# Gate weights split in their natural layout and turned by 48 DMA transposes instead of by TensorE

## The reference

```python
x = x + xattn(layernorm(x), ctx, Wq, Wkv)            # 128 context rows for each batch, one head of width 512
x = x + ffn(layernorm(x), w_gate, w_up, w_down)

def ffn(x, w_gate, w_up, w_down):                    # the inner width is 1536
    x = act_qdq(x)                                   # scale = max|x| / 32767 over the WHOLE tensor, round, clip
    up = act_qdq(x @ lpbq_dequant(w_up).T)
    gate = act_qdq(x @ lpbq_dequant(w_gate).T)       # weights: blocks of 32, 15 levels, dequantised
    sig = fixed_qdq_u16(sigmoid(gate))
    gate = act_qdq(gate * sig)
    o = act_qdq(gate * up)
    return o @ lpbq_dequant(w_down).T
```

## Time and profile before

| | us |
|---|---|
| three runs | 890.88, 889.6, 889.14 (median 889.6) |
| the profiled execution | 889.12 |
| its span | 887.3 |
| PE busy | 858.3 (97% of the span) |
| DVE, ACT, POOL busy | 689.5, 585.5, 195.4 |
| L1043, the gate matmuls, on the chain of waits | 130.05 to 316.69 |

### The profile page before, as it was taken

How to read it: one execution, slowest core, us unless ns; L and a number is a source line. 1 busy time by engine, 2 the same in 40 slices (tenths; PEclk the granted TensorE clock), 3 DMA queues, 4 the chain that set the end, 5 groups by cost and what they waited for, 6 DMA issues and landing times.

```text
span 887.3 us, 11953 instructions
## 1 busy us (share of the span) xinstructions
PE 858.3 (97%) x4108; PEld 424.5 (48%) x4108; DVE 689.5 (78%) x965; ACT 585.5 (66%) x712; POOL 195.4 (22%) x170
## 2 busy tenths in 40 slices
PE   7999969999999999999999999999899989999998
PEld 5877544444444444444444444444444434444443
DVE  4879885566647459689998987584999997999892
ACT  2468776785655366599999987752889965455430
POOL 0099948399300295000000000000000000000000
PEclk9999989999999999999999999999999999999999
DMA  9822228766989549999779964997998887989872
GB/s 348 339 84 109 107 83 288 232 169 188 304 252 313 196 156 238 270 379 371 261 258 341 334 236 161 357 378 262 323 406 271 277 319 273 374 299 401 316 294 96
DMA packets 118402, 236.56 MB, mean 267 GB/s; under 512 B 47952, under 2 KB 57168, under 8 KB 116304
## 3 DMA queue, kind: packets, MB, share of 16 engines
q1 hardware_dynamic: 117200, 231.77, 74.0%
q10 hardware_dynamic: 1152, 4.19, 1.2%
HBM read 130.55 MB, written 95.42 MB: 255 GB/s over the span
## 4 chain that ended last, share of the span: by engine, by line
PE 71%; DVE 9%; POOL 8%; issue 6%; DMA 3%; SPq 1%; ACT 1%; DVEq 0%; ACTq 0%; POOLq 0%
PE ps L1106 28%; PE ps L1043 21%; PE ps L1159 13%; PE ps L1059 4%; PE ps L1186 4%; DVE big L1960 3%; DVE big L1953 3%; POOL big L875 2%; DMA big<-in_L_ffn_w_gate_dram 2%; POOL big L832 1%; POOL big L826 1%; PE ps L1176 1%; POOL small L872 1%; DMA big<-up_park 1%; POOL big L830 1%
## 5 line engine op out<-in xcount | busy, mean ns | idle before, releaser
L1106 PE MATMUL ps<-big 128*128 (+1 forms) x1152 | 248.8, 379 | 0.0
L1204 ACT ACTIVATE big<-ps 128x1024 f32<-128x1024 f32 (+2 forms) x154 | 126.4, 830 | 147.7 <-PE ps L1043 62.5
L1043 PE MATMUL ps<-big 128*128 (+1 forms) x864 | 186.6, 379 | 0.7 <-DVE big L1736 0.7
L1106 PEld LDWEIGHTS ps<-big 128*128 128x128 f16 x1152 | 112.7, 98 | 135.9
L1043 PEld LDWEIGHTS ps<-big 128*128 128x128 f16 x864 | 84.4, 98 | 102.7 <-issue 0.9
L1159 PE MATMUL ps<-big 128*128 128x512 f16 x576 | 125.1, 379 | 3.2 <-DVE big L1981 3.2
L817 POOL PARTITION_ALL_REDUCE small<-small x8 | 2.9, 368 | 451.6 <-DVE small L1922 170.1
L1781 DVE TENSOR_REDUCE small<-big 128x1 f32<-128x1024 f32 x36 | 43.8, 1218 | 71.0 <-ACT big L1204 71.0
L1159 PEld LDWEIGHTS ps<-big 128*128 128x128 f16 x576 | 56.2, 98 | 71.6 <-issue 2.9
L1140 PE MATMUL ps<-big 128*128 128x512 f16 x384 | 84.2, 379 | 4.3 <-ACT big L1489 4.3
L1874 DVE TENSOR_REDUCE small<-big 128x1 f32<-128x1024 f32 x48 | 58.2, 1215 | 13.7 <-ACT big L1204 13.6
(11 more groups left out here) (118 smaller groups left out, 1222.3 us busy)
## 6 DMA issues: line engine op xcount, KB each, us to landing
big<-up_park SPq DMA_DIRECT2D x90, 512.0 KB, 6.7
big<-gate_park SPq DMA_DIRECT2D x48, 512.0 KB, 6.3
up_park<-big SPq DMA_DIRECT2D x48, 512.0 KB, 4.1
gate_park<-big SPq DMA_DIRECT2D x36, 512.0 KB, 2.7
sign_park<-big SPq DMA_DIRECT2D x36, 256.0 KB, 2.7
big<-in_x_dram SPq DMA_DIRECT2D x8, 1024.0 KB, 18.5
x_park<-big SPq DMA_DIRECT2D x8, 1024.0 KB, 3.9
product_park<-big SPq DMA_DIRECT2D x16, 512.0 KB, 3.5
```

The source lines that it names most:

```text
L1043: mm = nc.tensor.matmul(unit_banks(n)[:, j], WG[:, x, a, k % 2, o:o + P], XT[:, g, b, k], start=(k == 0 and a + b == 0), stop=(k == KC - 1 ...
L1106: mm = nc.tensor.matmul(ps[:, b + j], WU[:, a, t // 3, k, t % 3], XT[:, g, c, k], start=(k == 0 and a + c == 0), stop=(k == KC - 1 and c = ...
L1204: return nc.scalar.activation(dst, src, ACT.Copy)
```

## The change

The gate weights are no longer turned by PE. ACT and DVE split a chunk in its natural layout (`gate_rows_hi`, `gate_rows_lo`), chunks 0 to 9 in the attention's slots W_AT and the slots behind them, chunks 10 and 11 after `scale_late` on ACT and after the four pieces of group 0 on DVE. SP turns each chunk by four DMA transposes of 128 rows x 256 columns (two parts, two halves), between the stores of x, 48 in all. Chunks 0 to 8 count wg_turned, chunks 9 to 11 count wu_0. The load of the down weights, the first sums on POOL, the first unit of gate(0) and its unit 4 wait for these counts. The eighth call of `quant_weights` moves behind all_max(1), and the matmuls that only keep PE busy grow from 8 to 28 and move to the end of the attention.

```diff
-W_SLOT = NG * TI + PV_LAG
-W_BANK = (0, 1, 2, 3, 4, 5, 6, 2, 3, 4, 5, 6)
-W_ORDER = (2, 3, 4, 5, 6, 0, 1, 7, 8, 9, 10, 11)
-W_EARLY = 5
+W_AT = (12, 14, 14, 16, 20, 20, 23, 26, 26, 31)
+W_FIRST = 9
+WARM = 28
...
+        def gate_rows(l, c):
+            at = 38912 + 1536 * (c // 3 - 1) if c > 2 else HT0 + 12288
+            return part(at, 1536).bitcast(F16).rearrange("p (l n) -> p l n", l=2)[:, l, c % 3 * D:c % 3 * D + D]
...
+        W_MOST, W_LAST = 64 * W_FIRST, 64 * (OC - W_FIRST)
+        wu_turned, WU_TURNED = [wu_0, wg_ld[1], wn_ld[2], wd_turned], (W_LAST, 16, 16, 16 * 2 * KC)
...
+        def gate_turned(eng):
+            eng.wait_ge(wg_turned, W_MOST)
+            eng.wait_ge(wu_0, W_LAST)
...
-            with nc.sync.Fori(0, NG) as g:
+            def park_x2(g):
                 sp.wait_ge(x2_d_s, TI * g + TI)
                 sp.dma_start(x2_d[g], X[:, g].rearrange("p i d -> p (i d)")).then_inc(x2_st, 16)
 
-            sp.wait_ge(wt_lo, OC)
+            def turn_gate_weights(c):
+                sp.wait_ge(wt_lo, c + 1)
+                for l in range(2):
+                    for h in range(2):
+                        f = h ^ c % 2
+                        sp.dma_start(gate_weights(l, c)[:, h], gate_rows(l, c)[:, f * 256:f * 256 + 256],
+                                     transpose=True).then_inc(wg_turned if c < W_FIRST else wu_0, 16)
+
+            for g, cs in enumerate(((0,), (1, 2), (3,), (4, 5), (6,), (7, 8), (), (9,))):
+                for c in cs:
+                    turn_gate_weights(c)
+                park_x2(g)
+            for c in (10, 11):
+                turn_gate_weights(c)
+
+            gate_turned(sp)
             sp.dma_start(WN.rearrange("p (h n) -> p h n", h=KC),
                          wd_in.rearrange("(h p) n -> p h n", p=P)).then_inc(wn_ld[2], 16)
...
-                pool.wait_ge(wt_lo, OC)
+                gate_turned(pool)
...
+                if g == 6:
+                    pool.wait_ge(wg_turned, W_MOST)
...
-                if g < 5:
+                if g < 4:
                     quant_weights(g + 3, g + 3, 0)
             all_max(1, "hmx", "hall")
+            quant_weights(7, 7, 0)
...
-            for n in range(W_SLOT + OC):
+            for n in range(NT + PV_LAG):
...
-                    turn_weights(n - W_SLOT)
...
                     if isinstance(g, int) and g == 0:
-                        pe.wait_ge(wt_lo, (low_count(1), low_count(8), OC, OC, OC, OC)[n])
+                        if n == 0:
+                            pe.wait_ge(wg_turned, W_MOST)
+                        if n == W_FIRST // 2:
+                            pe.wait_ge(wu_0, W_LAST)
...
-            keep_warm(8, ident, P, 7)
+            pe.wait_ge(ht_ev, TI)
+            keep_warm(WARM, ident, P, 7)
+            pe.wait_ge(xt_ev, NT)
+            pe.wait_ge(exp_d, NT)
+            pe.wait_ge(x2_d_s, NT)
             gate(0)
...
-            def weights_hi(c, bank):
-                act.wait_ge(wt_mm, c + 1)
-                copy(gate_weights(0, c), ps[:, bank].rearrange("p (x k o) -> p x k o", x=2, k=2)).then_inc(wt_hi, 1)
+            def gate_rows_hi(c):
+                act.wait_ge(w_deq, (2 * c + 4) // 3)
+                if c > 2:
+                    act.wait_ge(wt_lo, c // 3 * 3)
+                copy(gate_rows(0, c), WN[:, c * D:(c + 1) * D]).then_inc(wt_hi, 1)
...
+                for c in range(len(W_AT)):
+                    if n == W_AT[c]:
+                        gate_rows_hi(c)
...
             h_int(1)
             for n in range(NT - TI, NT):
                 scale_late(n)
+            for c in range(len(W_AT), OC):
+                gate_rows_hi(c)
...
-            def weights_lo(c):
+            def gate_rows_lo(c):
 
                 dve.wait_ge(wt_hi, c + 1)
-                hi, lo = (gate_weights(l, c) for l in range(2))
-                nc.vector.tensor_tensor(lo, ps[:, W_BANK[c]].rearrange("p (x k o) -> p x k o", x=2, k=2), hi,
+                nc.vector.tensor_tensor(gate_rows(1, c), WN[:, c * D:(c + 1) * D], gate_rows(0, c),
                                         ALU.subtract).then_inc(wt_lo, 1)
...
-                if W_SLOT + 4 <= n < W_SLOT + 4 + W_EARLY:
-                    weights_lo(W_ORDER[n - W_SLOT - 4])
+                for c in range(len(W_AT)):
+                    if n == W_AT[c] + 1:
+                        gate_rows_lo(c)
...
-            for c in W_ORDER[W_EARLY:W_EARLY + 2]:
-                weights_lo(c)
...
-            for c in W_ORDER[W_EARLY + 2:]:
-                weights_lo(c)
+            for c in range(len(W_AT), OC):
+                gate_rows_lo(c)
```

More of the change, by code:

```diff
@@ L56 @@
 PAIR_AT = {NG * TI + X2_LAG + 1: 21, NG * TI + X2_LAG + 2: 23, NG * TI + X2_LAG + 5: 25, NG * TI + X2_LAG + 6: 27}
-def low_count(c):
-    return W_ORDER.index(c) + 1
 WTOP = (256.0, 2048.0, 2048.0)
@@ L363, in build @@
         w_blk, w_inv, w_rnd, w_deq = sem("w_blk"), sem("w_inv"), sem("w_rnd"), sem("w_deq")
-        wt_mm, wt_hi, wt_lo, wd_st = sem("wt_mm"), sem("wt_hi"), sem("wt_lo"), sem("wd_st")
+        wg_turned, wt_hi, wt_lo, wd_st = sem("wg_turned"), sem("wt_hi"), sem("wt_lo"), sem("wd_st")
         wu_0, wd_turned = sem("wu_turned"), sem("wd_turned")
-        wu_turned, WU_TURNED = [wu_0, wg_ld[1], wn_ld[2], wd_turned], (0, 16, 16, 16 * 2 * KC)
+        W_MOST, W_LAST = 64 * W_FIRST, 64 * (OC - W_FIRST)
+        wu_turned, WU_TURNED = [wu_0, wg_ld[1], wn_ld[2], wd_turned], (W_LAST, 16, 16, 16 * 2 * KC)
         s_raw, s_hi, s_lo = h2_d, pt_ev, ve1_d
@@ L1306, in _ @@
             take_xT(0)
-            for n in range(W_SLOT + OC + 1):
+            for n in range(NT + X2_LAG + 1):
                 if n + 1 < NT:
@@ L1318, in _ @@
                         centre(NT - TI + i)
-                if W_SLOT < n <= W_SLOT + OC:
-                    weights_hi(n - W_SLOT - 1, W_BANK[n - W_SLOT - 1])
+                for c in range(len(W_AT)):
+                    if n == W_AT[c]:
+                        gate_rows_hi(c)
                 if n % TI == 0 and TI <= n < NT + TI:
```

## The result

The changed kernel takes 911.17 us (median of 6 runs, 910.44 to 914.74), the kernel before 889.37 (median of 6, 888.23 to 890.88): a ratio of 1.0251, 95% interval 1.0232 to 1.027, slower. The forecast was 911.5 with a range of 899 to 919. The profiled execution of the changed kernel is the slowest of its six, 914.74 with a span of 912.9.

What follows compares the result with a forecast made beforehand. POOL's list bounds the stretch to 130 us, then PE, with gate(1) tied to the down weights' load. Profiled 889.1 + 20.6 for gate(1) starting later + 1.6 for the clock = 911.3; forecast 911.5, range 899 to 919.

Steps and rivals of the forecast that it cites:

- D: Attention: delay of the last variance, var2(7), by ACT's stand in slot 26 and DVE's ten subtractions; 1.8 to 8, taken 4 us.
- What it takes off POOL: POOL ahead of the maximum: one quant_weights of 4.9 us leaves, but the attention's variance limits the gain to 0.9 us.
- The maximum: POOL's maximum over partitions after the last normalise: at 130.25 instead of 127.15, from 120.5 + 4 + 5.76.
- The eighth quantisation: POOL behind the maximum: code change 7.42 and quantising 4.88, ending at 142.9; chunk 10 split by ACT and DVE at 144.2.
- The eight transposes: SP ahead of the down weights' load: 1.19 us each, 9.5 in all, plus 3.0 to land; load at 156.8, not 134.91.
- PE's unit 4: In gate(0), PE's unit 4 waits for the last chunks until 156.8: a stall of about 1 to 3 us, not deciding.
- The chain from the load to gate(1): From issuing the down weights' load to gate(1): 17.8 + 7.15, together 25.0 us; gate(1) at 181.8 instead of 161.15.
- The clock: PE after its idle time: granted clock falls to half for a stretch, costing 1.6 to 3.4 us; 1.6 taken.
- Nothing later is nearer: Behind gate(1): the down weights' quantisation shifts with what uses it, so no later stage adds delay.
- The rival of cheap transposes: SP: transposes cost about 0.4 us each like plain DMAs, load at about 150, kernel 903 to 905; chance 0.16.
- the faster one: SP's transposes are covered, last chunk landed by 137, gate(1) on time: 886.5 to 889 us; chance 0.06.

Runs made afterwards that it cites:

- quant_back: Changed kernel with the eighth quant_weights back ahead of the maximum and chunks 10 and 11 split in slots 40 and 41, 48 transposes kept: 897.46 us, ratio 1.0082.
- load_later: Changed kernel with the load of the down weights, and what DVE does with them, moved behind the transposes of groups 1 and 2: 905.2 us, ratio 1.0178.
- double_turn: Changed kernel with the eight transposes of chunk 10 issued a second time into unread memory, the load waiting for these too: 922.98 us, ratio 1.0367.
- warm64: Changed kernel with 64 instead of 28 groups of the matmuls that only keep PE busy: 913.73 us, ratio 1.0269.
- combo: quant_back with chunks 7 and 8 split in slot 28 instead of 26 and 64 instead of 28 keep-busy matmuls: 894.56 us, ratio 1.0064.

## Why the prediction was right, point by point

The mechanism, its place and its releaser came as predicted, and quant_back, load_later and double_turn show it by moving one part of it at a time. The terms that were off are D, the landing of the transposes, a stall that did not come, and a second clock term.

- *What it takes off POOL* (0.9 us): right. The last normalise ended 4.9 us behind the last variance before (121.40) and ends 4.1 us behind it now (127.06). D outweighs the gain.
- *D*: predicted 4 (1.8 to 8), measured 122.97 - 116.47 = 6.5, and 4.3 to 6.6 over the six kernels with this attention code. ACT's stand is 2.50 instead of 1.8, and the price of a subtraction is 0.78 in the mean, not 1.57: the ten take 7.6 us in the changed kernel. For the ten subtractions I counted DVE's own time; what I left out is POOL's, whose instructions grow beside them and make the sixth dequantisation 1.8 to 3.1 us later. The middle of a wide range was a choice, and this term has the largest error of the sum.
- *The maximum*: predicted 130.25, measured 133.00, D's error of 2.5 and a code change of 5.93 instead of 5.76.
- *The eighth quantisation*: from maximum to low part of chunk 10 predicted 13.95, measured 13.6 (146.6 - 133.00).
- *The eight transposes*: predicted 9.5 + 3.0, measured 158.09 - 146.64 = 11.45: 1.27 each to issue, and the last one lands 2.42 us after its issue began, 1.2 after it ended. The earlier trace rows counts the landing from the issue's start and I added it to the end: 3.0 where 1.2 was right, against 0.7 us too little for the issues. The choice of 1.19 over the half of it was right: a transpose of half the size costs SP the same. The Trainium skill, Advanced Engine Details and Errata, section X-Bar Transpose (TRN2), says that transpose DMAs are as fast as regular DMAs. At the issuing engine they aren't here: 1.247 us of SP in the median for 64 KB, against 0.33 to 0.58 for the plain DMAs L510, L547, L549 and L492 around them, and the measurement decides. The load went out at 158.09, predicted 156.8.
- *PE's unit 4* (a stall of 1 to 3 us): failed. Gate(0) began 2.7 us later than predicted and at half clock, and took 32.77 us, so the chunks were there. warm64 shows the stall, 1.44 us, where gate(0) is quick. It cost nothing either way.
- *The chain from the load to gate(1)*: predicted 25.0, measured 183.44 - 158.09 = 25.35. load_later shows that the transposes behind the load make it long. That the size is so near is in part luck. The integers made in unit 3 wait for the turned halves of group 1; in the kernel before these had landed at 152.0, 17.1 us after the load's issue and not 17.8 (again the landing counted from the issue's end), and ACT began the integers at 152.98 because it had waited for PE's unit 3 (150.97). So the load had about 2.0 us to spare, not 1.0. In the changed kernel PE had long done that unit; the halves landed at 176.0, 17.9 us after the load's issue, and the sign store released ACT at 175.09, so that both were ready for the integers at 176.05. My reading of the path was 0.7 us too long, the path then grew by 0.8, and the two cancel.
- *The clock* (1.6 in all): 1.7 at gate(0), which is hidden under the pause, and 1.5 at gate(1). The size that counts was right. That it falls twice was not in the sum.
- *Nothing later is nearer*: 1.1 us in the up stage is new. It isn't tied to the late load, since quant_back has it too and combo doesn't; its cause is open.

Term by term the profiled run gives 22.3 + 1.5 + 1.9 = 25.7, predicted 20.6 + 1.6 = 22.2. The median, 21.8, is nearer to the prediction than the terms are: the profiled run is 3.6 us above it. That 911.5 and 911.17 lie so close is therefore luck; the mechanism and the range aren't. The rival of cheap transposes falls with double_turn and L499's row, the faster one with the load at 158 where it had to be at 137. In quant_back the load goes out at 139.78, and the kernel is still slower than the one before, with gate(0) starting 5.7 us later (135.73 against 130.05).

## What to carry to other kernels

A queue's order is a dependence like any other: a load that is needed 25 us later must not stand behind transposes that wait for the slowest chain of the kernel. Before moving work off a critical engine, see what the engine waits for next (here the variance, 1.9 us behind) and what is issued behind the moved work on every queue. In the two sizes seen here DMA transposes are paid by their number, at the issuing engine. And a time that one trace shows for a stage (here D) should be looked up in a second kernel with the same code before a difference of 1 or 2 us is explained.

## What the runs showed that I had not expected

- A transposing DMA of 128 x 256 costs SP as much as one of 128 x 512: 1.18 us at least and 1.247 in the median against 1.19 and 1.27.
- In combo PE was kept busy until 2.63 us before gate(0), and the granted clock still fell to 0.69 in the window from 134 to 136, with PE busy again.
- Ten subtractions of 128 x 512 on DVE (7.6 to 9.7 us busy in the six kernels) delay the last variance by 1.6 to 3.9 us more than ten copies (5.7 us), and POOL's sixth dequantisation by 1.3 to 2.5 us. That ACT is the link between the two isn't shown: its idle time ahead of its own copies is 3.1 us in quant_back and 1.0 in quant_back_copy, but also 1.0 in load_later, with all ten subtractions.
- The same attention code ends its last variance at 120.8 to 123.1 in six kernels, a spread of 2.3 us.
